# Query rows interleaved by head in a transformer block: two swaps of 64 rows, weights split in that order

## The reference

```python
def apply_rope(t, pos):            # t: (b, heads, s, 64)
    ang = pos[:, None] * inv_freq[None, :]
    cos, sin = jnp.cos(ang), jnp.sin(ang)
    t1, t2 = t[..., :32], t[..., 32:]
    return concatenate([t1 * cos - t2 * sin, t1 * sin + t2 * cos], axis=-1)

q = (h @ Wq).reshape(b, s, 32, 64).transpose(0, 2, 1, 3)
k = (h @ Wk).reshape(b, s, 8, 64).transpose(0, 2, 1, 3)
v = (h @ Wv).reshape(b, s, 8, 64).transpose(0, 2, 1, 3)
q, k = apply_rope(q, pos), apply_rope(k, pos)
k, v = repeat(k, 4, axis=1), repeat(v, 4, axis=1)
out = softmax(causal(q @ k.T / 8)) @ v     # then @ Wo, residual, feed-forward
```

## Time and profile before

| what | value |
|---|---|
| median of 3 runs | 1933.71 us (1933.04 to 1939.78) |
| profiled execution, its own time | 1939.95 us |
| its span in the trace | 1938.1 us |
| PE busy | 1772.3 us, 91% |
| DVE busy | 1269.1 us, 65% |
| ACT busy | 1144.7 us, 59% |
| POOL busy | 964.6 us, 50% |

### The profile page before, as it was taken

How to read it: one execution, slowest core, us unless ns; L and a number is a source line. 1 busy time by engine, 2 the same in 40 slices (tenths; PEclk the granted TensorE clock), 3 DMA queues, 4 the chain that set the end, 5 groups by cost and what they waited for, 6 DMA issues and landing times. The chain is left out here.

```text
span 1938.1 us, 28246 instructions
## 1 busy us (share of the span) xinstructions
PE 1772.3 (91%) x9585; PEld 1423.4 (73%) x9585; DVE 1269.1 (65%) x2079; ACT 1144.7 (59%) x2307; POOL 964.6 (50%) x773
## 2 busy tenths in 40 slices
PE   8579999999999999999999999985999599999997
PEld 7367777777777778778777777764888478787876
DVE  6358788778888788788777878783233345444443
ACT  3257777777777877778777777783223243323221
POOL 0127576666666666666765666651000044444443
PEclk8789999999999999999999999997999799999999
DMA  7034353344344343344444433426555200101000
GB/s 258 12 93 114 85 135 108 90 129 110 88 126 109 94 124 101 109 115 108 117 106 102 120 98 91 129 77 225 174 174 176 95 1 1 50 1 50 1 28 22
DMA packets 174922, 190.97 MB, mean 99 GB/s; under 512 B 31408, under 2 KB 117688, under 8 KB 174784
## 3 DMA queue, kind: packets, MB, share of 16 engines
q1 hardware_dynamic: 137792, 140.99, 25.5%
q10 hardware_dynamic: 36992, 48.25, 8.9%
HBM read 86.12 MB, written 31.74 MB: 61 GB/s over the span
## 5 line engine op out<-in xcount | busy, mean ns | idle before, releaser
L814 DVE TENSOR_TENSOR p_lo<-ps_b,p_hi 128x512 fp32r<-128x512 f32 x576 | 395.5, 687 | 193.1 <-ACT p_hi L740 189.0
L753 ACT ACTIVATE p<-ps_b,negm 128x640 f32<-128x640 f32 (+7 forms) x512 | 381.5, 748 | 114.0 <-DVE negm L822 111.3
L740 ACT CAST p_hi<-ps_b 128x512 fp32r<-128x512 f32 x576 | 336.8, 588 | 158.3 <-PE ps_b L682 155.5
L822 DVE TENSOR_REDUCE negm<-ps_b 128x1 f32<-128x640 f32 (+7 forms) x512 | 376.3, 745 | 40.0 <-PE ps_b L674 39.3
L682 PE MATMUL ps_b<-ident,p 128*128 128x128 f32 x2304 | 350.0, 274 | 3.2 <-DVE p_lo L814 2.1
L672 PE MATMUL ps_b<-k_hh,q_hl 128*128 128x512 f32 (+3 forms) x768 | 272.5, 355 | 39.2 <-ACT p L753 36.2
L694 PE MATMUL ps_b<-p_hi,v_hl 128*128 128x512 f32 x576 | 276.7, 480 | 16.3 <-ACT o_sb L746 16.0
L682 PEld LDWEIGHTS ps_b<-ident,p 128*128 128x128 f32 x2304 | 258.7, 141 | 37.3 <-DVE p_lo L814 5.3
L673 PE MATMUL ps_b<-k_l,q_hl 128*128 128x512 f32 (+3 forms) x768 | 258.3, 349 | 0.0
L695 PE MATMUL ps_b<-p_lo,v_hl 128*128 128x512 f32 x576 | 227.7, 395 | 0.0
L672 PEld LDWEIGHTS ps_b<-k_hh,q_hl 128*128 128x128 f32 x768 | 146.5, 191 | 88.4 <-ACT p L753 55.4
(11 more groups left out here) (139 smaller groups left out, 3251.4 us busy)
## 6 DMA issues: line engine op xcount, KB each, us to landing
rot_x<-rot_s SPq DMA_DIRECT2D x320, 64.0 KB, 2.0
q_hl<-rot_s SPq DMA_DIRECT2D x128, 128.0 KB, 2.5
q_hl<-rot_x SPq DMA_DIRECT2D x128, 128.0 KB, 2.5
rd_all<-reciprocals SPq DMA_DIRECT2D x128, 128.0 KB, 3.1
o_low<-o_sb ACTq DMA_DIRECT2D x128, 128.0 KB, 2.4
attention_out<-o_sb SPq DMA_DIRECT2D x128, 128.0 KB, 2.5
o_raw<-attention_out SPq DMA_DIRECT2D x32, 512.0 KB, 4.8
wf<-in_L_ffn_w_gate_up ACTq DMA_DIRECT2D x32, 256.0 KB, 3.1
```

The costliest lines, as they stand in the source:

```text
L740: act.copy(p_hi[:, T % P_RING, :], ps[:, T_BANK + T % 2, :]).then_inc(phi_ready, 1)
L753: act.activation(p_32[:, parity, h, column * P:column * P + nk], s, ACT.Exp, bias=negm[:, k:k + 1], scale=1.0, accum_out=den[:, parity, k: ...
L814: dve.tensor_tensor(p_lo[:, T % P_RING, :], ps[:, T_BANK + T % 2, :], p_hi[:, T % P_RING, :].bitcast(F32), ALU.subtract).then_inc(plo_read ...
L822: dve.tensor_reduce(negm[:, k:k + 1], s, AX.X, ALU.max, negate=True).then_inc(max_ready, 1)
```

## The change

Query rows are interleaved by head: row 2e + h of the bank is element e of head h. So both heads' first halves are rows 0 to 63 and the second halves rows 64 to 127, and the swap for a query use takes two DMAs of 64 rows. To get that order, the weight columns of a head pair are read in the order (element, head) by ACT and DVE when they split the weights: each split is three instructions of 512 columns, two that read `w_raw` with a hop of 64 words at each element, and one for keys and values that reads a plain run. `w_hi` and `w_lo` are written in plain runs. The placing DMAs read every second row (`src[h:P:2]`). `cos` and `sin` are stored interleaved; keys keep their order and get tables of their own, `k_cos` and `k_sin`, 64 rows each, which are two more loads in the prologue.

```diff
+    k_cos, k_sin = np.tile(cos, (2, 1)), np.concatenate([sin, -sin], 0)
+    return np.repeat(k_cos, 2, 0), np.repeat(k_sin, 2, 0), k_cos, k_sin
...
-        buf_swap = [Events(swapped[i], [32 if X_USES[n][0] == "kv" else 64 for n in BUF[i]], BUF_HERE[i]) for i in range(2)]
+        buf_swap = [Events(swapped[i], [32] * len(BUF[i]), BUF_HERE[i]) for i in range(2)]
...
+        splits_hi, splits_lo = [Events(s, [3], 0) for s in (whi_ready, w_ready)]
...
+        def by_head(w, hp):
+            return w[:, :, hp * P:hp * P + P].rearrange("p k (h e) -> p k e h", h=2)
+
+        def by_pair(w, hp):
+            return w[:, :, hp * P:hp * P + P].rearrange("p k (e h) -> p k e h", h=2)
...
             def swap(g, n):
-                kind, buf = X_USES[n][0], buf_of(n)
+                buf, rows = buf_of(n), D // 2 if X_USES[n][0] == "kv" else D
                 uses_done.await_(sp, g, n)
-                for i in range(2 if kind == "kv" else 4):
-                    sp.dma_start(rot_x[32 * i:32 * i + 32, buf, :],
-                                 rot_s[32 * (i ^ 1):32 * (i ^ 1) + 32, buf, :]).then_inc(swapped[buf], 16)
+                for near, far in ((0, rows), (rows, 0)):
+                    sp.dma_start(rot_x[near:near + rows, buf, :], rot_s[far:far + rows, buf, :]).then_inc(swapped[buf], 16)
...
-                                     src[half[h], buf, :].rearrange("p (q c) -> p q c", q=2)).then_inc(q_placed[buf], 16)
+                                     src[h:P:2, buf, :].rearrange("p (q c) -> p q c", q=2)).then_inc(q_placed[buf], 16)
...
-                    act.copy(w_hi[:], w_raw[:]).then_inc(whi_ready, 1)
+                    for hp in range(2):
+                        act.copy(by_pair(w_hi, hp), by_head(w_raw, hp)).then_inc(whi_ready, 1)
+                    act.copy(w_hi[:, :, GQ * D:], w_raw[:, :, GQ * D:]).then_inc(whi_ready, 1)
...
-                    dve.tensor_tensor(w_lo[:], w_raw[:], w_hi[:].bitcast(F32), ALU.subtract).then_inc(w_ready, 1)
+                    for hp in range(2):
+                        dve.tensor_tensor(by_pair(w_lo, hp), by_head(w_raw, hp), by_pair(w_hi, hp).bitcast(F32),
+                                          ALU.subtract).then_inc(w_ready, 1)
+                    dve.tensor_tensor(w_lo[:, :, GQ * D:], w_raw[:, :, GQ * D:], w_hi[:, :, GQ * D:].bitcast(F32),
+                                      ALU.subtract).then_inc(w_ready, 1)
...
-                for dst, src in ((cos, cos_in), (sin, sin_in), (mask, mask_in)):
+                for dst, src in ((cos, cos_in), (sin, sin_in), (k_cos, k_cos_in), (k_sin, k_sin_in), (mask, mask_in)):
                     sp.dma_start(dst[:], src).then_inc(consts_in, 16)
```

More of the change, by code:

```diff
@@ L340, in load_weights, with attention @@
         sp.dma_start(w_raw[:, :, at:at + n], src[bass.ds(g, 1)].rearrange("g p k n -> (g p) k n")).then_inc(w_in, 16)
-def attention(nc, wq, wk, wv, w_gu, w_p, consts_in, w_in, w_raw, cos, sin, mask, ident, hT_hi, hT_lo, ot_dram, rden_dram,
-              tern_gu, tern_p):
+def attention(nc, wq, wk, wv, w_gu, w_p, consts_in, w_in, w_raw, cos, sin, k_cos, k_sin, mask, ident, hT_hi, hT_lo, ot_dram,
+              rden_dram, tern_gu, tern_p):
     with ExitStack() as ctx:
@@ L594, in step @@
                     swap(g, n)
-                for g, n, _ in body.uses(T, 10, kinds=("qx", "qy")):
+                for g, n, _ in body.uses(T, PLACE_AT, kinds=("qx", "qy")):
                     place(g, n)
@@ L782, in step @@
                     exponentials(g, r)
-                for g, n, _ in body.uses(T, 8, kinds=("kv",)):
+                for g, n, _ in body.uses(T, SPLIT_AT, kinds=("kv",)):
                     _, unit, part, _ = X_USES[n]
@@ L827, in rotary_products @@
                 uses_x.await_(dve, g, n)
-                rows = D if kind == "kv" else P
                 if kind == "kv":
-                    out = [r[0:rows, buf, :] for r in (rot_c, rot_s)]
-                    src = ps[0:rows, X_BANK, :]
-                    by = [t[0:rows, kv_cols(part)] for t in (cos, sin)]
+                    rows, by = slice(0, D), [t[:, kv_cols(part)] for t in (k_cos, k_sin)]
+                    out = [r[rows, buf, :] for r in (rot_c, rot_s)]
+                    src = ps[rows, X_BANK, :]
                 else:
+                    by = [quarters(t[:], kind) for t in (cos, sin)]
                     out = [r[:, buf, :].rearrange("p (q c) -> p q c", q=2) for r in (rot_c, rot_s)]
                     src = ps[:, X_BANK, :].rearrange("p (q c) -> p q c", q=2)
-                    by = [quarters(t[:], kind) for t in (cos, sin)]
                 dve.tensor_tensor(out[0], src, by[0], ALU.mult)
```

29 lines of the change are left out of this document (16 added, 13 removed).

## The result

| | before | after |
|---|---|---|
| median of 7 runs each | 1933.71 us (1932.98 to 1939.78) | 1947.7 us (1943.07 to 1948.82) |
| ratio after to before | | 1.0065, interval 1.0054 to 1.0075 |
| profiled execution, its own time | 1939.95 us | 1948.82 us |
| its span | 1938.1 us | 1947.0 us |

A forecast was written before the change was run, and what follows sets the result against it. PE bounds the body (96% busy), a chain of latencies the start-up. Eight splits at 1.68 us, 13.4, less 2.1 gained at start-up: +11.3 us, so 1945 us, own range 1941 to 1951, full range 1931 to 1952.

The forecast's parts named there:

- The sum for a split: At each of 8 weight splits: 0.33 us for more instructions, 0.75 DVE hop, 0.60 ACT hop, together 1.68 us lost.
- The place on the path: At all 8 splits, every us added to ACT's or DVE's part was counted as lost time.
- PE's first product would wait for `w_lo`: Sign in later groups: PE's first product starts with this wait, and all that follows is 1.7 us later a group.
- The hop on DVE: In DVE's split: two subtractions reading with a jump take 0.375 us more each, 0.75 us a split.
- the row for `a_lo`: DVE subtraction from SBUF, 679 ns best, 1054 mean, 1773 worst; its mean over best sized the hop at 0.375 us.
- The hop on ACT: In ACT's split: hopping reads slowed by DVE's share, 0.7 of ACT's own rate, 0.60 us a split.
- Three instructions instead of one: At each split: added instructions cost 0.20 us on ACT and 0.13 on DVE, together 0.33 us.
- The swap in the body: In attention's body: shorter swaps cut POOL's wait but gain nothing, at most 0.8 us of DVE.
- The start-up, a gain of 2.1 us: Before the first score: swap used 0.9 us earlier, two issues fewer on SP save 1.24; bounds 0 and 3 us.
- the forecast 111.3: Sign in the start-up: first score at 111.75 + 1.7 - 2.1 = 111.3 us.
- which I had kept as a bound: Lower bound of the start-up gain: nothing, if reading every second row makes placings that much slower.
- Two more loads, nothing: In the prologue: loads of `k_cos` and `k_sin` fall in SP's idle gap and cost nothing; without it 1 us.

The follow-up runs named there:

- the last experiment: The changed kernel with DVE's three subtractions of a split one step earlier (W_LOW = 28 instead of 29): 1951.66 us, ratio to before 1.0092.
- the run with ACT's pieces alone: The kernel before with only ACT's cast to `w_hi` in three plain pieces of 512 columns, DVE's subtraction left whole: 1933.72 us, ratio 1.0000.
- DVE's three alone: The kernel before with only DVE's subtraction to `w_lo` in three plain pieces of 512 columns, ACT's cast left whole: 1949.85 us, ratio 1.0072.

## Why the prediction was right, and where it was not

**The time.** 1945.0 was forecast, 1947.7 measured, and the forecast's own range of 1941 to 1951 holds it. The sum for a split was 1.68 us; the durations at a later split grew by 1.69 (0.43 on ACT, 1.26 on DVE). The stretch over it on PE grew by 1.47. But the terms inside are not those that I wrote, and that two sums agree to 0.01 us is chance.

**The place on the path: right.** `w_lo`, `p_lo` and `negm` stand in one queue on DVE, with a margin of 0.05 us to PE. The forecast that PE's first product would wait for `w_lo` and that all behind it would be later came true, seven times, and the last experiment confirms it from the other side. ACT's part is on the path too, by PE's wait for `o_sb`, but a later wait can take some of it back: of the 0.18 us in the run with ACT's pieces alone nothing reached the end of the stretch.

**The hop on DVE, 0.75 us a split: failed.** The pieces with a hop take 695 ns, not 1070. The Trainium skill has an exception for this in "Vector Engine (DVE) Microarchitecture Reference", section 5.2: the single read stream of an operation with one source, which alternates between two regions 16 KiB apart and writes one word for two read, was measured at the full rate. The trace agrees with it in a case that the page does not have, two sources, a word written for each element, and regions 256 bytes apart: 695 against 690 ns. Over four regions the trace agrees with that section's general rule, 1.73 ns a column for a source that hops at every element against 1.054, or 0.68 more, beside 0.75 measured. I took the general rule's side by the row for `a_lo`. That row is no reading with a hop at all: its operands lie plainly in SBUF, both of them, and its spread from 679 to 1773 is the same 1.1 us as a held piece here (0.68 and 1.77). The trace of the kernel before shows that it is the hold. Of its 64 instances the 49 that take 0.98 us or more all begin while an instruction of POOL is under way, and of the 15 at 0.69 or less 13 meet none. The other two run inside an instruction of POOL that itself lasts 3.62 us instead of some 1.1, so there it was POOL that stood. One of the slowest, which ends 0.54 us behind POOL's:

```profile
1698.48 1.62 POOL L1384 TENSOR_TENSOR ssq<-ssq,sq 128x512 f32<-128x512 f32 x1
...
1698.87 1.77 DVE L1452 TENSOR_TENSOR a_lo<-a,a_hi 128x512 fp32r<-128x512 f32 x1
```

**The hop on ACT, 0.60 us a split: mis-sized.** Measured 2 x 0.125 = 0.25 us, and together with two more instructions the cast goes from 1.39 to 1.82 us (178.91 to 180.73), 0.43 instead of 0.80. The two more instructions were sized well, 0.18 in the run with ACT's pieces alone where 0.20 was forecast, though that run's time shows no loss.

**Three instructions instead of one, 0.13 us on DVE: the step that failed most.** The cost of an instruction was counted as its own fixed time. It was not counted that a gap between two instructions lets another engine in. In place of the 0.13 stands a hold of 1.08 us on DVE, of which 0.95 reaches PE. The Trainium skill states the rule in "SBUF — State Buffer", section "SBUF: two separate sides": the port pair that VectorE and GpSimd share is locked by whichever starts first, for its whole instruction; it concerns DVE instructions with two SBUF inputs, if GpSimd's reads SBUF, and those in a two-port mode. The trace agrees: POOL 2.87 instead of 1.28 us before, DVE 2.84 instead of 1.75 where POOL starts 0.09 us earlier. I had weighed pages on how a port streams and not the one on who shares it, and had not read POOL's row at 189.31.

**The swap in the body, nothing: right in the sum, wrong in the reason.** The row for the wait of POOL was read as covered, since no PE wait ended on POOL. Through the port POOL does act on DVE. Sooner swaps move POOL's additions, and with them which DVE instruction is held: in the kernel before with two swaps `w_lo` is held in six splits where it was in none, at 0.9 us each; with four swaps in the changed kernel more pieces are held.

**The rest of the loss, not in the sum.** 5.8 us come from the stretch from the 65th to the 72nd product, and `above` is what turns the hold into lost time there. Once it is on ACT that stretch is even. Why the changed kernel meets the hold there more often than the one before isn't shown: with two swaps and one `w_lo` that stretch loses nothing, nor does it with three plain pieces on both engines, and with DVE's three alone it loses 2.9 us.

**The start-up, a gain of 2.1 us: the mechanism right, the size open.** The swap was used 0.8 us sooner after its issue (0.9 forecast), and SP's issues took 1.33 less (1.24 forecast). The split cost less there than the 1.68 of the sum: from the first `w_hi` to the end of `w_lo` it took 3.91 us instead of 3.36, 0.55 more, with POOL idle. The first score at 109.33 instead of the forecast 111.3 looks like more. But attention began 0.7 us earlier (the first `w_hi` at 64.51 instead of 65.21), and the profiled execution of before had a longer start than others of its kind: from `w_hi` to the first score it took 46.5 us, and 44.8 to 46.0 in four runs with the same four swaps (both splits, ACT's alone, DVE's alone, `above` given to ACT); the changed kernel took 44.8, and the kernel before with two swaps 43.9. The clock had its part in the profiled pair, behind the first score. From 112 to 120 us PE's granted clock was 0.50 before (the level of 1.2 GHz) and 0.95 after, by the view of busy time by stretch, before's row first:

```profile
112.00:120.00 8.00, 7.40 (x19) 4.67 (x19) 4.60 (x5) 2.43 (x5) 1.28 (x1) 0.50 0.41 98
```

```profile
112.00:120.00 8.00, 5.95 (x28) 4.00 (x27) 4.64 (x5) 5.67 (x11) 2.58 (x2) 0.95 0.34 90
```

With the same four swaps, both the run with both splits in plain pieces and the kernel before with `above` on ACT had 1.00 there, so the lower level is not the swaps' doing. The two profiled executions overstate the gain. The placing was slower by reading every second row, which I had kept as a bound. These are the issues of after (KB each, median us to landing); before they were 2.0, 2.5 and 2.5:

```profile
rot_x<-rot_s SPq DMA_DIRECT2D x128, 128.0 KB, 2.4
q_hl<-rot_s SPq DMA_DIRECT2D x128, 128.0 KB, 3.1
q_hl<-rot_x SPq DMA_DIRECT2D x128, 128.0 KB, 3.2
```

**Two more loads, nothing: nothing speaks against it.** Attention began no later.

## What to carry to other kernels

Look, before an instruction of VectorE with two SBUF operands is split, moved or added, at what GpSimd does in the same microseconds, and look for rows of both engines that last longer than their shortest: min, median and max of one line differing by 1.1 us was the sign here. One long instruction can be cheaper than three short ones although the sum of their own times differs by 0.1 us, because each gap is a door for the other engine. And an engine for which nobody waits is not harmless: what makes GpSimd earlier can make VectorE later, and a cheap 8-column instruction in the wrong place (`above`, 0.16 us) was worth more than the whole change once it was taken off that queue.

## What the hardware showed that I had not expected

- A VectorE subtraction with both operands in SBUF and a GpSimd addition do not overlap: the later one stands until the other ends (2.84 for 1.75 us on DVE, 2.69 to 2.89 for 1.28 on POOL). `p_lo` and the rotary products, which read one operand from PSUM, kept their 0.68 us. This is `p_lo` in the kernel before, ns min/median/max; 440 of the 576 ran beside an instruction of POOL:

```profile
L814 DVE TENSOR_TENSOR p_lo<-ps_b,p_hi x576: 671/691/694, 128.4 to 1308.9; 128x512 fp32r<-128x512 f32 x192
```

- A product of 8 columns with a single SBUF operand was held as well: 1.10 us for 0.16.
- A hop between two regions 256 bytes apart was free on DVE (695 against 690 ns for 512 columns) and cost 0.13 us on ACT; over four regions it cost 0.75 ns a column on DVE and 0.94 on ACT.
- A placing of 128 KB that reads every second row took 3.1 us to land where 64 adjacent rows took 2.5.
